# One core, attention and experts: single score banks, a fourth maxima bank, and the row maxima transposed on VectorE

## The chip, the cores and the metric

The kernel runs on 1 core of one Trainium2 chip. Its time is the device time of one execution in microseconds (us). Before the change it takes 2506.57 us, the median of 3 runs (2504.11 to 2506.87). The engines are TensorE (PE in the profile), VectorE (DVE), ScalarE (ACT), GpSimd (POOL) and SyncE (SP), which issues most DMAs. PEld is TensorE's weight load.

## The reference, cut to what matters

The input x is 8 sequences of 1024 tokens with 256 features. It is normalised, goes through attention with 16 heads of 16 features (with a linear position bias) and through a mixture of 8 experts (two per token) plus a shared one, and everything is added to x:

```
xn = layernorm(x)
scores = einsum('bqhd,bkhd->bhqk', Q, K) * scale + alibi
attn = softmax(scores); out = einsum('bhqk,bkhd->bqhd', attn, V) @ Wo + bo
y = sum over the two best experts of w * (silu(xn @ W1) * (xn @ W2)) @ W3  + shared expert
result = x + out + y
```

All of it is float32 with a softmax that subtracts each query's largest score.

## The kernel before, in words

The program is one list of steps (class `Order`), and each engine walks the same list and emits its own part of each step. So the order of `Order.run` and `Order.attention` is the order of every queue. Between engines there are semaphores only.

Stages: layernorm and the projections (to about 210 us), attention (to about 1530 us), the experts in 71 blocks of 256 slots (to about 2130 us), then the shared expert and the output.

Attention goes over 64 pairs of heads (8 sequences, 8 pairs). A pair takes 4 rows of `ORDERS`, one for every two chunks of 128 keys. In a row, `S` is a score matmul (a chunk of 128 keys against 512 queries of one head, with the bias and the negative row maximum as extra contraction rows), `u` a maxima matmul (128 queries against 512 keys), and `P` a third of the values matmuls of the row before. S and u of neighbouring positions use different halves of TensorE's rows and run beside each other. Per pair there are 32 S, 32 u and 12 P.

The maxima run ahead of the scores by `AHEAD` units, because a query's largest score must be known before its exponentials. VectorE reduces each u (`reduce_max`, 128x512 to 128x1, L944), then folds the 32 numbers of a pair to 16 (L948); GpSimd negates them and splits them in a high and a low part (L1215 to L1220, tile `mneg`, 128x32). `max_rows` brings these 128x32 numbers to rows 52 and 53 of each head's query operand `QO`: TensorE transposes them (L503) into a score bank, ScalarE copies them out to `mT` (L788), and SyncE issues two DMAs of 16 pieces of 512 B (L1399). The first S of the next pair waits for these DMAs (semaphores `mx0`, `mx1`).

PSUM has 8 banks of 512 columns. Before, banks 0 to 3 hold scores in two groups of two (both heads; ScalarE takes 1024 columns in one exponential, L799), bank 4 the values, banks 5 to 7 the maxima.

SyncE's queue in a pair, in order: `sq<-accs` (L1410, waits for ScalarE's copy of the last pair's values, L806, at the end of row 0), the 12 loads of the operands of the pair three later (L1389) and their 4 bias rows (L1393), `OTd<-accs` (L1422), the maxima's DMAs (L1399), `Sd<-sq` (L1414), and after that has landed `asum<-Sd` (L1418).

In pairs 0 to about 25 VectorE has two more steps a pair for the routing of tokens. In pairs 34 to 49 GpSimd scatters the tokens with indirect DMAs.

Of the kernel before, what the change touches and what calls it, by code (L numbers as in the profile page):

```python
# [36 lines left out]
AHEAD = 52  # L37
# [6 lines left out]
ORDERS = ("SuSuSuPSuSuSuPSuSuP", "SuSuSuPSuSuPSuSuSuP", "SuSuPSuSuSuPSuSuSuP", "SuSuPSuSuSuPSuSuSuP")  # L44
# [9 lines left out]
    "xt qkmm vmm mxmm mrt smm pv rtmm sct gmm up down sdn "  # L54

    "wsplh woh xh qkh vev mrev exp acc1 rte wsh sch sg hh yev och "

    "wspll bq wol st ag ve norm xl qkl mxred m16 rcp rt rtm rtd rtw rts rtp rtc wslv scl hf hl ocl s1 gf fin "
# [17 lines left out]
class Order:  # L76
# [3 lines left out]
    def run(self):  # L80
# [17 lines left out]
        for g in range(NG):  # L98
# [29 lines left out]
            if n >= 32 and not rows0:  # L128
                self.max_rows(0, 7)
                rows0 = True  # L130
# [80 lines left out]
    def attention(self, s, n):  # L211

        r, kc = divmod(s, 8)
        if s % 2 == 0:
            i = v = 0
            for c in ORDERS[kc // 2]:
                if c == "S":
                    if r < NPAIR:
                        self.scores(r, kc + i // 4, i % 2, i // 2 % 2)
                    i += 1  # L220
                elif c == "u":
                    if n < 32 * NPAIR:
                        self.max_unit(n)
                        n += 1
                else:
                    if v == 1 and kc == 4 and r + 1 < NPAIR:
                        self.max_rows(r + 1)
                    if s >= 2:
                        self.values(*divmod(s - 2, 8), v)
                    v += 1  # L230
# [6 lines left out]
        if s % 2 and s // 2 < NBLK:  # L237
            self.clear_slots(s // 2, 16 * r + 2 * kc)
        if SCAT_AT <= r < SCAT_AT + NG:
            self.scatter_rows(r - SCAT_AT, kc, 16 * r + 2 * kc)  # L240
# [34 lines left out]
    def max_rows(self, r, bank=None): pass  # L275
# [29 lines left out]
class Ring(Order):  # L305
# [14 lines left out]
    def bank(self, what, i):  # L320
        return 5 + self.turns.index((what, i)) % 3
# [10 lines left out]
def build(nc, t, out):  # L332
    ctx = ExitStack()
    with ctx:
# [43 lines left out]
        mT = sbuf(ctx, "mT", [32, 2, P], F32R)  # L378
# [106 lines left out]
        class Tensor(Order):  # L485
# [57 lines left out]
            def ring_bank(self, what, i):  # L543

                at = ring.turns.index((what, i))
                if at >= 3:
                    was, j = ring.turns[at - 3]
# [4 lines left out]
                else:  # L552
                    self.w.wait_ge("vev", 4 * NG)
                    if at == 2:
                        self.w.wait_ge("mxred", ring.turns[0][1])
                return 5 + at % 3

            def max_unit(self, n, bank=None):
                r, u = divmod(n, 32)
                hh, i, half = 1 - u % 2, u // 4, u // 2 % 2  # L560
# [4 lines left out]
                else:  # L565
                    self.w.wait_ge("mxred", n)
                    if n >= 32:
                        self.w.wait_ge("mrev", 1)
# [3 lines left out]
            def max_rows(self, r, bank=None):  # L572
                self.w.wait_ge("mnl", r + 1)
                self.w.wait_ge("c_ident", 16)
                if bank is None:
                    bank = 1
                    self.w.wait_ge("exp", 16 * (r - 1) + 9)
                else:
                    self.w.wait_ge("mxred", 32)
                self.turn(ps[0:32, bank, 0:P],  # L580
                          mneg[:, r % 2, :, :, :].rearrange("p h l i -> p (h l i)")).then_inc(sem["mrt"], 1)

            def scores(self, r, kc, hh, half):
                k, h0, n = r % 4, 64 * hh, 16 * r + 2 * kc + half
                bank = 2 * (n % 2) + hh
                self.w.wait_ge(f"op{k}", 256 * (r // 4 + 1))
                self.w.wait_ge(f"mx{r % 2}", 32 * (r // 2 + 1))
                if n < 2:
# [3 lines left out]
                if kc == 5 and half == 0 and hh == 1:  # L592
                    self.w.wait_ge("mrev", min(r + 2, NPAIR))
                q = self.mm(ps[:, bank, :], KO[h0:h0 + KEXP, k, kc * P:(kc + 1) * P],
                            QO[h0:h0 + KEXP, k, half * GT:(half + 1) * GT], True, True)
                if hh == 1:
                    q.then_inc(sem["smm"], 1)

            def values(self, r, kc, v):
# [3 lines left out]
                for c in range(kc, kc + 2):  # L603
# [4 lines left out]
                    self.w.wait_ge("exp", n + 2)  # L608
                    self.w.wait_ge("vcp", 2 * b + 2)
                    if c == 0:  # L610
                        self.w.wait_ge("acc1", r)
                        self.w.wait_ge("vev", 4 * NG)
                    for hh in range(2):
                        for half in range(2):
                            g4 = 2 * hh + half
                            done = self.mm(ps[32 * g4:32 * g4 + 32, 4, at],
                                           vb[:, b % 2, c, 32 * (2 * j + hh):32 * (2 * j + hh) + 32],
                                           pt(n + half)[:, hh * GT:(hh + 1) * GT][:, at], c == 0 and v == 0,
# [16 lines left out]
            def slot_columns(self, b):  # L635
                k = b % 2
                self.w.wait_ge(f"xs{b % 4}", 16 * (b // 4 + 1))
                if b < 2:
                    self.w.wait_ge("exp", 16 * NPAIR)
# [11 lines left out]
            def block_up(self, b, hc):  # L651
# [8 lines left out]
                if n < 4:  # L660
                    self.w.wait_ge("exp", 16 * NPAIR)
# [78 lines left out]
        class Scalar(Order):  # L740
# [43 lines left out]
            def max_rows(self, r, bank=None):  # L784
                bank = 1 if bank is None else bank
                self.w.wait_ge(f"mx{r % 2}", 32 * (r // 2))
                self.w.wait_ge("mrt", r + 1)
                self.e.copy(mT[:, r % 2, :], ps[0:32, bank, 0:P]).then_inc(sem["mrev"], 1)  # L788

            def scores(self, r, kc, hh, half):  # L790
                if hh == 0:
                    return
                n = 16 * r + 2 * kc + half
                b = 2 * (n % 2)
                if n % NPT >= NPT // 2:
                    projections_over(self.w)
                self.w.wait_ge("pv", n // 2 - 3)
                self.w.wait_ge("smm", n + 1)
                self.e.activation(pt(n), ps[:, b:b + 2, :], ACT.Exp).then_inc(sem["exp"], 1)  # L799

            def values(self, r, kc, v):
                if kc == 6 and v == 2:
# [3 lines left out]
                    self.e.copy(accs[:, r % 2, :], ps[:, 4, :]).then_inc(sem["acc1"], 1)  # L806
# [67 lines left out]
        class Vector(Order):  # L874
# [648 lines left out]
```

## Time and profile before

| | |
|---|---|
| median of 3 runs | 2506.57 us |
| the profiled execution's own time | 2505.09 us |
| its span | 2503.3 us |
| PE busy | 2456.3 us (98%) |
| DVE busy | 2052.1 us (82%) |
| ACT busy | 1658.8 us (66%) |
| POOL busy | 843.7 us (34%) |
| chain that ended last | PE 93%, ACT 3%, issue 1%, DVE 1%, DMA 1% |
| granted TensorE clock, mean | 0.993 |

Busy time is the union of an engine's instruction spans. TensorE's matmuls overlap and their ends are modelled, so its busy share near 100% doesn't say that it ran without waits; the start-to-start times in the timeline say more. A timeline's row stands for several like instructions in a row, with the start of the first, the time from there to the end of the last, and their count.

### The profile page before, as it was taken

The page shows a single profiled execution, that of the slowest core. Times are in us where ns is not written, and L with a number is a line of the kernel's source. Part 1 is how long each engine was busy: PE and PEld are TensorE (multiplying, and loading weights), DVE is VectorE, ACT ScalarE, POOL GpSimd, SP SyncE. Part 2 cuts the span into 40 slices and gives each one's busy share as a digit, 9 for nine tenths or more (in the row PEclk, how much of TensorE's full clock was granted, in tenths as well). Part 3 has the DMA queues.
Part 4 walks back from the last instruction along what each step waited for, and adds up shares of the span by engine and source line. Part 5 has one row for each costly group of instructions (what it writes and reads, how often), then busy time and mean ns, then how long its engine had stood idle before and what let it go on. Part 6 is the DMA issues. An engine that isn't in the chain of part 4 may idle for free.

```text
span 2503.3 us, 51165 instructions
## 1 busy us (share of the span) xinstructions
PE 2456.3 (98%) x20186; PEld 1649.2 (66%) x20186; DVE 2052.1 (82%) x3521; ACT 1658.8 (66%) x2314; POOL 843.7 (34%) x929
## 2 busy tenths in 40 slices
PE   6999999999999999999999998999999999999999
PEld 5775444444444444444444445999999988888887
DVE  7977999999999999999999993777777765554444
ACT  3445777787788888888888887777777753333222
POOL 3332332332101115555411112333333334444444
PEclk9998999999999999999999999999999999999999
DMA  8985443544222235555422233777777743444332
GB/s 285 339 298 177 153 142 122 161 145 140 76 68 78 80 85 160 157 154 154 147 76 76 75 118 105 237 237 239 239 241 241 242 152 102 121 117 116 102 102 85
DMA packets 213599, 384.41 MB, mean 154 GB/s; under 512 B 45444, under 2 KB 134724, under 8 KB 203988
## 3 DMA queue, kind: packets, MB, share of 16 engines
q1 hardware_dynamic: 175088, 218.25, 28.3%
q0 software_dynamic: 37184, 162.09, 20.4%
q8 instruction: 160, 2.62, 0.4%
q10 hardware_dynamic: 1088, 0.79, 0.1%
q14 instruction: 79, 0.65, 0.1%
HBM read 249.10 MB, written 141.49 MB: 156 GB/s over the span
## 4 chain that ended last, share of the span: by engine, by line
PE 93%; ACT 3%; issue 1%; DVE 1%; DMA 1%; SPq 0%; POOL 0%; ACTq 0%; DVEq 0%; POOLq 0%
PE ps L490 91%; PE ps L503 3%; ACT pta L799 1%; ACT ptb L799 0%; ACT mT L788 0%; DMA Wvst<-in_Wg 0%; ACT qkH L775 0%; SPq L1389 0%; DVE qkL L934 0%; DMA xr<-Xn 0%; DVE xn L918 0%; DVE XL L926 0%; DMA OPS<-Alid 0%; POOL vs L1183 0%; DVE VB L1083 0%
## 5 line engine op out<-in xcount | busy, mean ns | idle before, releaser
L944 DVE TENSOR_REDUCE mx<-ps 128x1 f32<-128x512 f32 x2048 | 1262.0, 680 | 34.6 <-PE ps L490 19.0
L490 PE MATMUL ps<-OPS 52*128 52x512 f32 (+1 forms) x4096 | 821.2, 452 | 9.5 <-ACT pta L799 1.8
L490 PEld LDWEIGHTS ps<-OPS 54*128 54x128 f32 (+1 forms) x4096 | 426.4, 186 | 507.9 <-issue 203.9
L799 ACT ACTIVATE pta<-ps 128x1024 f32<-128x1024 f32 x512 | 510.4, 1023 | 150.8 <-PE ps L490 143.4
L799 ACT ACTIVATE ptb<-ps 128x1024 f32<-128x1024 f32 x512 | 510.9, 1024 | 116.5 <-PE ps L490 116.2
L490 PE MATMUL ps<-OPS,WB 128*128 128x256 f32 (+1 forms) x2268 | 363.5, 312 | 2.9 <-DVE VB L1083 1.6
L490 PEld LDWEIGHTS ps<-OPS,WB 128*128 128x128 f32 x2268 | 310.5, 180 | 32.3 <-issue 3.3
L490 PE MATMUL ps<-pta,VB 128*32 128x352 f32 (+1 forms) x4096 | 302.6, 390 | 0.0
L490 PE MATMUL ps<-ptb,VB 128*32 128x352 f32 (+1 forms) x4096 | 301.4, 389 | 0.0
L1227 POOL TENSOR_TENSOR accs<-accs,asum 128x512 f32<-128x512 f32 x64 | 81.7, 1277 | 586.7 <-DMA asum<-Sd 561.6
L490 PE MATMUL ps<-OPS,WB0c 128*128 128x256 f32 (+3 forms) x1440 | 257.9, 330 | 3.8 <-issue 2.8
L490 PEld LDWEIGHTS ps<-OPS,WB0c 128*128 128x128 f32 (+1 forms) x1440 | 210.2, 181 | 33.8 <-issue 4.6
L490 PE MATMUL ps<-WB,OPS 128*128 128x256 f32 (+1 forms) x1422 | 188.1, 283 | 0.0
L1088 DVE TENSOR_TENSOR OPS<-VB,OPS 128x256 fp32r<-128x256 f32 (+1 forms) x213 | 151.2, 710 | 33.6 <-ACT OPS L841 33.6
L490 PEld LDWEIGHTS ps<-WB,OPS 128*128 128x128 f32 (+1 forms) x1422 | 178.4, 191 | 0.1
L865 ACT ACTIVATE VB<-ps 128x512 f32<-128x512 f32 (+1 forms) x96 | 57.0, 594 | 174.1 <-PE ps L490 174.1
L490 PEld LDWEIGHTS ps<-pta,VB 128*32 128x32 f32 x4096 | 94.1, 109 | 99.8 <-issue 84.2
L490 PEld LDWEIGHTS ps<-ptb,VB 128*32 128x32 f32 x4096 | 94.2, 109 | 99.6 <-issue 90.3
L871 ACT CAST OPS<-VB 128x512 fp32r<-128x512 f32 (+1 forms) x96 | 59.6, 621 | 138.2 <-DVE VB L1112 138.2
L1309 POOL DMA_INDIRECT gath<-Ys,slot x128 | 132.9, 1038 | 36.4 <-issue 34.1
L841 ACT CAST OPS<-VB 128x256 fp32r<-128x256 f32 (+1 forms) x213 | 86.5, 406 | 83.6 <-DVE VB L1083 83.4
L1267 POOL DMA_INDIRECT Xs<-xr,slot x128 | 125.8, 983 | 44.5 <-PE ps L490 25.2
(155 smaller groups left out, 2755.0 us busy)
## 6 DMA issues: line engine op xcount, KB each, us to landing
OPS<-QKh SPq DMA_DIRECT2D x512, 64.0 KB
Xs<-zero POOLq DMA_DIRECT2D x71, 256.0 KB, 3.3
xr<-Xs SPq DMA_DIRECT2D x71, 256.0 KB, 5.3
Ys<-VB SPq DMA_DIRECT2D x71, 256.0 KB, 5.0
QKh<-qkH SPq DMA_DIRECT2D x16, 1024.0 KB, 7.2
QKl<-qkL SPq DMA_DIRECT2D x16, 1024.0 KB, 8.9
OPS<-QKl SPq DMA_DIRECT2D x256, 64.0 KB
asum<-Sd SPq DMA_DIRECT2D x64, 256.0 KB
```

The lines of the kernel that those rows point to most:

```text
L490: return self.e.matmul(o, l, r, start=start, stop=stop)
L503: return self.e.transpose(o, in_, ident[:, :])
L799: self.e.activation(pt(n), ps[:, b:b + 2, :], ACT.Exp).then_inc(sem["exp"], 1)
L841: self.e.copy(HH[0:hn, s, 0:BT], hfq[0:hn, k, :]).then_inc(sem["hh"], 1)
L865: self.e.activation(sg[0:hn, k, :], ps[0:hn, 2 + 2 * (n % 2), :], ACT.Silu).then_inc(sem["sg"], 1)
L871: self.e.copy(HH[0:hn, s, :], hf[0:hn, k, :]).then_inc(sem["hh"], 1)
L944: e.reduce_max(mx[:, k2, hh, i, half:half + 1], ps[:, bank, :], AX.X).then_inc(sem["mxred"], 1)
L1088: e.tensor_tensor(HL[0:hn, s, 0:BT], hfq[0:hn, k, :], HH[0:hn, s, 0:BT].bitcast(F32), ALU.subtract).then_inc(sem["hl"], 1)
L1227: self.e.tensor_tensor(accs[:, r % 2, :], accs[:, r % 2, :], asum[:, :], ALU.mult).then_inc(sem["nrm"], 1)
L1267: e.indirect_dma_start(Xs[:, :], bass.IndirectOffsetOnAxis(ap=slot[:, c, 4 * g + j:4 * g + j + 1], axis=0), xr[:, k, j, :], None).then_inc ...
L1309: self.e.indirect_dma_start(gath[:, j, c, :], None, Ys[:, :], bass.IndirectOffsetOnAxis(ap=slot[:, c, i:i + 1], axis=0)).then_inc(sem[f"ga ...
```

## The change

- The scores use three single banks, 0 to 2. Each S has its own semaphore count and its own exponential of 512 columns, so there are 2048 exponentials where there were 1024, and S number n waits for the exponential of n-3.
- The values move to bank 3, the maxima get banks 4 to 7.
- The order in a row: S now goes through a head's two query halves first and then to the other head; u the same the other way round. One `ORDER` for all four rows in place of four. `AHEAD` goes from 52 to 56.
- Of a pair's 16 couples of u, four (`DOUBLE`) are reduced over two neighbouring banks in one instruction, 128x1024 to 128x2.
- The transposition of `mneg` goes from TensorE and ScalarE to VectorE (`transpose`, 32x32 blocks, SBUF to SBUF), at the first P of the third row where it was the second. The result lies in four blocks of partitions, so that SyncE issues eight DMAs of 16 pieces of 128 B in place of two of 16 pieces of 512 B.

```
-ORDERS = ("SuSuSuPSuSuSuPSuSuP", "SuSuSuPSuSuPSuSuSuP", "SuSuPSuSuSuPSuSuSuP", "SuSuPSuSuSuPSuSuSuP")
+ORDER = "SuSuSuPSuSuSuPSuSuP"
+DOUBLE = (2, 6, 10, 14)
...
-                        self.scores(r, kc + i // 4, i % 2, i // 2 % 2)
+                        self.scores(r, kc + i // 4, i // 2 % 2, i % 2)
...
-                    if v == 1 and kc == 4 and r + 1 < NPAIR:
+                    if v == 0 and kc == 4 and r + 1 < NPAIR:
                         self.max_rows(r + 1)
...
-        mT = sbuf(ctx, "mT", [32, 2, P], F32R)
+        mT = sbuf(ctx, "mT", [P, 2, 32])
...
             def scores(self, r, kc, hh, half):
...
-                self.w.wait_ge("exp", n - 1)
...
+                self.w.wait_ge("exp", n - 2)
+                self.mm(ps[:, n % 3, :], KO[h0:h0 + KEXP, k, kc * P:(kc + 1) * P],
+                        QO[h0:h0 + KEXP, k, half * GT:(half + 1) * GT], True, True).then_inc(sem["smm"], 1)
...
-                self.e.activation(pt(n), ps[:, b:b + 2, :], ACT.Exp).then_inc(sem["exp"], 1)
+                self.e.activation(pt(m)[:, half * GT:(half + 1) * GT], ps[:, n % 3, :], ACT.Exp).then_inc(sem["exp"], 1)
...
+                if u // 2 not in DOUBLE or n < AHEAD:
+                    self.w.wait_ge("mxmm", n + 1)
+                    self.e.reduce_max(mx[:, r % 2, hh, i, half:half + 1], ps[:, bank, :], AX.X).then_inc(sem["mxred"], 1)
+                elif half:
+                    self.w.wait_ge("mxmm", n + 1)
+                    self.e.reduce_max(mx[:, r % 2, hh, i, :], ps[:, bank - 1:bank + 1, :], AX.X).then_inc(sem["mxred"], 2)
...
+            def max_rows(self, r):
+                self.w.wait_ge("mnl", r + 1)
+                self.w.wait_ge(f"mx{r % 2}", 128 * (r // 2))
+                self.e.transpose(mT[:, r % 2, :], mneg[:, r % 2, :, :, :].rearrange("p h l i -> p (h l i)")
+                                 ).then_inc(sem["mtr"], 1)
...
-            def max_rows(self, r, bank=None):
-                self.w.wait_ge("mrev", r + 1)
+            def max_rows(self, r):
+                self.w.wait_ge("mtr", r + 1)
                 for hh in range(2):
-                    self.e.dma_start(QO[64 * hh + 52:64 * hh + 54, r % 4, :].bitcast(F32).rearrange("l (i n) -> l i n", n=P),
-                                     mT[16 * hh:16 * hh + 16, r % 2, :].bitcast(F32)).then_inc(sem[f"mx{r % 2}"], 16)
+                    for b in range(4):
+                        c0 = 32 * b + 16 * hh
+                        self.e.dma_start(QO[64 * hh + 52:64 * hh + 54, r % 4, :].bitcast(F32)
+                                         .rearrange("l (i b n) -> l b i n", i=8, b=4)[:, b, :, :],
+                                         mT[c0:c0 + 16, r % 2, :]).then_inc(sem[f"mx{r % 2}"], 16)
```

On SyncE, in the middle of attention, the queue before, from the last loads of a pair to the first of the next (`OPS` is the tile that holds `QO`):

```order
L1389 DMA OPS<-QKh 16x1024 x4
L1389 DMA OPS<-QKl 16x1024 x2
L1393 DMA OPS<-Alid 2x1024 x2
L1422 DMA OTd<-accs 128x512
L1399 DMA OPS<-mT 2x8x128 x2
L1414 DMA Sd<-sq 128x16
L1418 DMA asum<-Sd 128x1x512
L1410 DMA sq<-accs 128x1x16
```

And the same stretch of SyncE's queue now:

```order
L1374 DMA OPS<-QKh 16x1024 x4
L1374 DMA OPS<-QKl 16x1024 x2
L1378 DMA OPS<-Alid 2x1024 x2
L1410 DMA OTd<-accs 128x512
L1386 DMA OPS<-mT 2x8x32 x8
L1402 DMA Sd<-sq 128x16
L1406 DMA asum<-Sd 128x1x512
L1398 DMA sq<-accs 128x1x16
```

The maxima's DMAs stand at the same place, behind the loads and `OTd<-accs`; there are eight where there were two, and each keeps its 16 pieces.

On VectorE, a pair in the second half of attention before (`mx` takes the reductions, `m` the fold to 16, `sq` belongs to the sums of the softmax):

```order
L948 TENSOR_REDUCE m<-mx 128x16
L944 TENSOR_REDUCE mx<-ps 128x1 x12
L953 RECIPROCAL sq<-sq 128x16
L944 TENSOR_REDUCE mx<-ps 128x1 x20
L948 TENSOR_REDUCE m<-mx 128x16
```

And a pair now:

```order
L932 STREAM_TRANSPOSE mT<-mneg 128x32
L919 TENSOR_REDUCE mx<-ps 128x1
L922 TENSOR_REDUCE mx<-ps 128x2
L919 TENSOR_REDUCE mx<-ps 128x1 x2
L938 RECIPROCAL sq<-sq 128x16
L919 TENSOR_REDUCE mx<-ps 128x1 x4
L922 TENSOR_REDUCE mx<-ps 128x2
L919 TENSOR_REDUCE mx<-ps 128x1 x6
L922 TENSOR_REDUCE mx<-ps 128x2
L919 TENSOR_REDUCE mx<-ps 128x1 x2
L926 TENSOR_REDUCE m<-mx 128x16
```

The fold moves to the end of a pair's first row, four units earlier against the scores; one transposition is new; and of each row's eight units the fifth and sixth are one instruction.

## Rows read from the trace of the kernel before

**Rows 1.** The page, part 1: busy time and share of the span
```profile
PE 2456.3 (98%) x20186; PEld 1649.2 (66%) x20186; DVE 2052.1 (82%) x3521; ACT 1658.8 (66%) x2314; POOL 843.7 (34%) x929
```
**Rows 2.** Timeline of PE, 800 to 840 us: start, length, engine, instructions, count
```profile
804.87 1.24 PE L490 MATMUL ps<-OPS 54*128 54x512 f32 x6
806.04 0.80 PE L490 MATMUL ps<-ptb,VB 128*32 128x352 f32 x8
806.77 1.08 PE L490 MATMUL ps<-OPS 54*128 54x512 f32 x6
807.78 0.75 PE L490 MATMUL ps<-ptb,VB 128*32 128x160 f32 x16
808.46 0.74 PE L490 MATMUL ps<-OPS 54*128 54x512 f32 x4
809.13 0.80 PE L490 MATMUL ps<-ptb,VB 128*32 128x352 f32 x8
...
817.26 0.28 PE L503 MATMUL ps<-ident,mneg 128*32 128x128 f32 x1
817.47 0.75 PE L490 MATMUL ps<-ptb,VB 128*32 128x160 f32 x16
...
825.06 1.25 PE L490 MATMUL ps<-OPS 54*128 54x512 f32 x6
```
**Rows 3.** Timeline of DVE, 800 to 840 us
```profile
800.65 12.24 DVE L944 TENSOR_REDUCE mx<-ps 128x1 f32<-128x512 f32 x20
812.92 0.19 DVE L948 TENSOR_REDUCE m<-mx 128x16 f32<-128x32 f32 x1
813.03 7.73 DVE L944 TENSOR_REDUCE mx<-ps 128x1 f32<-128x512 f32 x12
820.67 0.24 DVE L953 RECIPROCAL sq<-sq 128x16 f32<-128x16 f32 x1
```
**Rows 4.** Timeline of DVE, 821.9 to 822.5 us
```profile
821.38 1.27 DVE L944 TENSOR_REDUCE mx<-ps 128x1 f32<-128x512 f32 x2
```
**Rows 5.** Timeline of ACT, 808 to 812 us
```profile
810.16 0.58 ACT L806 COPY accs<-ps 128x512 f32<-128x512 f32 x1
810.64 1.03 ACT L799 ACTIVATE ptb<-ps 128x1024 f32<-128x1024 f32 x1
```
**Rows 6.** Timeline of SP, 810 to 843 us: its DMA issues
```profile
810.77 0.57 SPq L1410 DMA_DIRECT2D sq<-accs  x1
...
814.22 0.57 SPq L1393 DMA_DIRECT2D OPS<-Alid  x2
814.83 2.91 SPq L1389 DMA_DIRECT2D OPS<-QKh  x4
...
819.71 1.36 SPq L1399 DMA_DIRECT2D OPS<-mT  x2
...
835.10 1.92 SPq L1389 DMA_DIRECT2D OPS<-QKh  x4
...
839.00 1.37 SPq L1399 DMA_DIRECT2D OPS<-mT  x2
```
**Rows 7.** SP's waits, 740 to 900 us: us in total, times, longest
```profile
SPq L1418 <- DMA Sd<-sq: 13.1, 8, 2.6
```
**Rows 8.** SP's waits, 900 to 1250 us
```profile
SPq L1418 <- DMA Sd<-sq: 35.4, 18, 3.0
```
**Rows 9.** Line 1399: issue time in ns (min/median/max), first and last start
```profile
L1399 SPq DMA_DIRECT2D OPS<-mT x128: 616/654/810, 173.7 to 1504.5; - x128
```
**Rows 10.** DVE's groups by shape, whole run: busy us, mean ns of one
```profile
L974 DVE TENSOR_TENSOR r_o<-r_t,r_r 128x512 f32<-128x512 f32 x2 | 1.4, 680 | 0.0
...
L926 DVE TENSOR_TENSOR XL<-ps,XH 128x1024 fp32r<-128x1024 f32 x16 | 19.4, 1212 | 5.4 <-ACT XH L766 5.4
```
**Rows 11.** Timeline of DVE, 236 to 282 us, pairs with routing steps
```profile
253.06 0.24 DVE L953 RECIPROCAL sq<-sq 128x16 f32<-128x16 f32 x1
...
274.43 0.24 DVE L953 RECIPROCAL sq<-sq 128x16 f32<-128x16 f32 x1
```

More of the change, by code:

```diff
@@ L35 @@
 EPS = 1e-5
-AHEAD = 52
+AHEAD = 56
 FIRST = 5
@@ L127, in run @@
                 self.spread_v(0, g - V_AT)
-            if n >= 32 and not rows0:
-                self.max_rows(0, 7)
+            if n >= 36 and not rows0:
+                self.max_rows(0)
                 rows0 = True
@@ L215, in attention @@
             i = v = 0
-            for c in ORDERS[kc // 2]:
+            for c in ORDER:
                 if c == "S":
                     if r < NPAIR:
-                        self.scores(r, kc + i // 4, i % 2, i // 2 % 2)
+                        self.scores(r, kc + i // 4, i // 2 % 2, i % 2)
                     i += 1
@@ L274, in max_unit, with max_rows @@
     def max_unit(self, n, bank=None): pass
-    def max_rows(self, r, bank=None): pass
+    def max_rows(self, r): pass
     def load_v(self, b, f): pass
@@ L320, in bank @@
     def bank(self, what, i):
-        return 5 + self.turns.index((what, i)) % 3
+        return 4 + self.turns.index((what, i)) % 4
 def rows(w):
@@ L545, in ring_bank @@
                 at = ring.turns.index((what, i))
-                if at >= 3:
-                    was, j = ring.turns[at - 3]
+                if at >= 4:
+                    was, j = ring.turns[at - 4]
                     if was == "max":
@@ L615, in values @@
                             g4 = 2 * hh + half
-                            done = self.mm(ps[32 * g4:32 * g4 + 32, 4, at],
+                            done = self.mm(ps[32 * g4:32 * g4 + 32, 3, at],
                                            vb[:, b % 2, c, 32 * (2 * j + hh):32 * (2 * j + hh) + 32],
-                                           pt(n + half)[:, hh * GT:(hh + 1) * GT][:, at], c == 0 and v == 0,
+                                           pt(n + hh)[:, half * GT:(half + 1) * GT][:, at], c == 0 and v == 0,
                                            c == 7 and v == 2)
@@ L782, in project_v @@
                 self.e.copy(vs[:, k, j, :], ps[:, bank, 0:D + NE]).then_inc(sem["vev"], 1)
[L784 to L788, printed above, removed]
-            def scores(self, r, kc, hh, half):
[L791 to L795, printed above, removed]
+            def scores(self, r, kc, hh, half):
+                m, n = 16 * r + 2 * kc + hh, 32 * r + 4 * kc + 2 * hh + half
+                if m % NPT >= NPT // 2:
                     projections_over(self.w)
-                self.w.wait_ge("pv", n // 2 - 3)
+                self.w.wait_ge("pv", m // 2 - 3)
                 self.w.wait_ge("smm", n + 1)
-                self.e.activation(pt(n), ps[:, b:b + 2, :], ACT.Exp).then_inc(sem["exp"], 1)
+                self.e.activation(pt(m)[:, half * GT:(half + 1) * GT], ps[:, n % 3, :], ACT.Exp).then_inc(sem["exp"], 1)
             def values(self, r, kc, v):
@@ L805, in values @@
                     self.w.wait_ge("pv", 8 * (r + 1))
-                    self.e.copy(accs[:, r % 2, :], ps[:, 4, :]).then_inc(sem["acc1"], 1)
+                    self.e.copy(accs[:, r % 2, :], ps[:, 3, :]).then_inc(sem["acc1"], 1)
             def route(self, i):
```

61 lines of the change are left out of this document (20 added, 41 removed).

## The prediction

> **What bounds the kernel now.** I read the page's busy shares first: PE 98% and DVE 82% over the whole span, ACT 66% [rows 1]. They mix stages. The change touches attention alone, so I went to one pair of heads in the timelines. PE begins the first S of a pair at 804.87 and of the next at 825.06 [rows 2]: a period of 20.2 us, 64 times.
>
> What each engine needs in it, by start-to-start times:
>
> - PE [rows 2]: a P of 352 columns takes 0.73 (806.04 to 806.77), six matmuls without a wait 1.01 (806.77 to 807.78), a P of 160 columns 0.68, four matmuls 0.67 (808.46 to 809.13). A row is 2 x 1.01 + 0.67 + 2 x 0.73 + 0.68 = 4.83, a pair 19.3, and the transposition 0.2 (817.26 to 817.47): 19.5.
> - DVE [rows 3]: 20 reductions in 12.27 (800.65 to the fold at 812.92, 0.61 each), the fold 0.11, 12 reductions in 7.64 (0.64 each), the reciprocal 0.16: 20.2, the whole period. DVE has no gap. But two reductions in a row that nothing holds last 1.27, of which the second's own length is 0.68 [rows 4]: 0.59 from start to start, 0.60 in round numbers. So 32 of them need 19.2, and some 0.7 us a pair are small waits for PE, too short to show as gaps since neighbouring spans overlap.
> - ACT: 16 exponentials of 1024 columns and a copy; it idles a third of the span [rows 1].
>
> So the period is DVE's, with PE 0.7 behind and small waits between them. It is so in the pairs with routing too: the reciprocals at 253.06 and 274.43 lie 21.4 apart [rows 11], and two more steps of up to 0.68, as this one [rows 10], stand in each.
>
> The reader should then look at a queue that no busy share shows: SP's. After `sq<-accs` (810.77, which waits for ACT's copy that ended at 810.74 [rows 5]) SP issues 12 loads, 4 bias rows and `OTd<-accs` without pause, and reaches the maxima's two DMAs at 819.71, and in the next pair at 839.00 [rows 6]. They hold it 1.36 together. The first S of the next pair waits for them to land. No row has that landing; the nearest is `Sd<-sq`, also 8 KB, whose landing SP waits for 13.1 us in 8 times, 1.6 each [rows 7], and 35.4 in 18, 2.0 each, while GpSimd scatters [rows 8]. So they land at 821.07 + 1.6 = 822.7, 2.4 us before S at 825.06; in the next pair at 840.37 + 1.6 = 842.0, 3.2 us before S at 825.06 + 20.2. That spare time, 2.8 us on average, is what the change meets.
>
> **The change part by part.**
>
> Eight DMAs for two on SP. Six more, in the one place where everything behind is waited for. One costs what it holds SP: 0.62 to 0.81, median 0.65 [rows 9], and 1.36 for two with the gap, so 0.69 each with the next gap. The new ones have a quarter of the bytes and the same 16 pieces from 16 partitions into 2. Bounds: the cheapest issue on SP's queue is a bias row pair, 0.57 for two or 0.28 each [rows 6]; the dearest of L1399 is 0.81 [rows 9]. I take 0.69, since pieces, partitions and direction stay and only the length of a piece shrinks. Six more: 6 x 0.69 = 4.1 us. Less the spare 2.8, S comes 1.3 late. Row 0 gives back about 0.2: it needs 4.83 where it takes 4.99 now (804.87 to 809.13 and a P of 0.73 [rows 2]), and the copy waits behind an exponential of half the length. So the period is 20.2 + 1.3 - 0.2 = 21.3. This is a closed loop (S, row 0, copy, SP's queue, DMAs, S), so the delay comes back in every pair and can't be worked off by what runs ahead. In the scatter stage landing is 0.4 longer: 21.7. The one load group of 2.91 where its like takes 1.92 (814.83, 835.10) [rows 6] is in the averages; six more instructions on the queue, if such holds come by instruction, add 0.1.
>
> [...]
>
> DVE. Four couples a pair in one instruction. The nearest rows are a 128x512 operation of 0.68 and a 128x1024 one of 1.21 [rows 10]: 0.53 per 512 columns, so a double takes 0.60 + 0.53 = 1.13 for 1.20, 0.07 saved, 0.3 a pair. Bounds: nothing, and 0.60 each if the second bank were free, 2.4 a pair. The Trainium skill's price for one DVE access to PSUM (Perfetto Trace Analysis, Optimizing Scalar/DVE Operations) is about 125 ns, which would make it 0.5 a pair; the measured start-to-start less the columns' 0.53 leaves 0.07 here. Added is the transposition, 32 columns: between the fold's 0.11 and the reciprocal's 0.24 [rows 3], taken as 0.13. DVE's need is 24 x 0.60 + 4 x 1.13 + 0.11 + 0.16 + 0.13 + 0.1 (the fold waits for the last reduction) = 19.4. Beside a period of 21.3 none of it counts.
>
> PE. The transposition goes, 0.2 a pair, and its wait. The order of S and u still gives each position both halves of the array; I cost it at nothing, bounds -0.1 and +0.1 a row. PE's own need is 19.3, hidden too.
>
> ACT. 32 exponentials of 512 columns. A 512-column copy takes 0.48 to the next start (810.16 to 810.64) [rows 5], so 15.4, and 0.48 for the copy: 15.9 of 21.3. Hidden; upper bound 0.58 each, the copy's full length, 18.6 with the copy, hidden still. Three single banks: an S writes about 0.5, is read 0.58, and its bank is due again 1.7 us later (two groups on), so no wait there.
>
> A fourth maxima bank removes most of the small waits between PE and DVE, 0.5 a pair, and `AHEAD` 56 puts four more reductions ahead of the first S, 4 x 0.6 = 2.4 us once, of which DVE's later lead gives nothing back when SP bounds. At the end 56/32 pairs run without maxima; there single banks let S and exponentials overlap where groups of two alternate: 0 to 20.2 - 15.9 = 4.3 a pair, 0 to 7.5 in all, 4 taken.
>
> The transposition's wait for GpSimd's `mnl` holds DVE's queue, but the fold is 2 rows earlier, so it is over. It runs 11 to 12 us after the pair's start, before SP is there (13.9 to 14.8 us).
>
> **The sum**, against the profiled execution (2505.09):
>
> - 18 pairs outside routing and scatter: 18 x 1.1 = +20.
> - 19 pairs with scatter or other bulk traffic (34 to 50, and 60 and 61, where the experts' first loads begin): 19 x 1.5 = +28.
> - 24 pairs with routing, period 21.4 now, 21.3 by the loop, DVE 19.4 + 1.2 = 20.6: 0.
> - more holds on the queue, 37 x 0.1 = +4; start +2; end -4.
>
> Together +50: 2555 by the profiled execution, 2556 by the median, which is 1.5 above it.
>
> **Rivals.**
>
> A. The short DMAs are cheap to issue (like the bias rows, 0.28, 0.33 with the gap). Then 6 x 0.33 - 2.8 is below nothing, the loop isn't closed, and the period is PE's and DVE's: 19.4, with some waits 19.6. 37 x 0.6 + 24 x 0.7 + 4 - 2 = 41 gained: 2465. At 0.42, as a load of 16 pieces (four in 1.92 [rows 6] at the most 0.48 each with the gap), 8 issues take 3.7 and the period is about 19.6 to 20: 2480. [...] Against: L1399 held SP 0.62 even at its least [rows 9]. The change is slower than now from about 0.55 an issue on, and that is the point that decides between the sides.
>
> B. Break-even: issues of 0.5 to 0.55 eat just what DVE and PE gain: 2495 to 2515.
>
> C. The landing grows as well, since eight small DMAs queue behind each other and behind the scatter's traffic (longest wait 3.0 against 2.0 on average [rows 8]): 1 us more in 61 pairs, 2615.
>
> D. The loop is as forecast, but the copy and the loads start later than now because a stalled PE restarts at a lower clock. Nothing in the rows speaks for it; I leave it in C's chance.
>
> **How the numbers follow.** Forecast 0.72, A 0.15, B 0.06, C and D 0.07. The forecast's own range is 2530 to 2590: issue 0.65 to 0.75 with its gap, landing 1.3 to 2, which is 0.5 a pair either way in 61 pairs. With the others the range is 2490 to 2600. This kernel's measurement can tell 0.2% (5 us) from no change. Faster by more: A and half of B, 0.17. Within: 0.03. Slower: 0.80.
>
> **What would show it.** In the profile after: eight `OPS<-mT` issues of about 0.65 in a row, some 5.5 us; PE's first S of a pair waiting for the DMA, with 1 to 2 us idle, in pairs of about 21.3; DVE's busy share in attention down from 98% to near 90%; double reductions of about 1.21 length; exponentials of about 0.6. It would be wrong if the eight take under 4 us, or if the period is below 20 with DVE without gaps; and the loop would be wrong if PE waits for maxima or exponentials instead.

## The result, and the profile after

The changed kernel takes 2536.73 us, the median of 4 runs (2527.61 to 2542.31), where the kernel before, run beside it, takes 2505.34 (2502.41 to 2506.87). The ratio is 1.0123, with a 95% interval of 1.0091 to 1.0156: slower, as forecast (2556, range 2490 to 2600), though by 31 us and not by 50. The profiled execution took 2534.91 us, its span is 2532.7, and the granted TensorE clock is 0.982 on average where it was 0.993.

The page, part 1, answers to [rows 1]; part 4 is the chain that ended last, first by engine and then by line; the last row is the score and maxima matmuls' group of part 5:

```profile
PE 2418.7 (95%) x20122; PEld 1590.6 (63%) x20122; DVE 2027.7 (80%) x3336; ACT 1711.2 (68%) x3274; POOL 841.3 (33%) x929
...
PE 58%; SPq 27%; DMA 5%; ACT 4%; issue 4%; DVE 2%; POOL 0%; ACTq 0%; DVEq 0%; POOLq 0%
PE ps L491 55%; SPq L1374 12%; SPq L1386 10%; DMA OPS<-mT 5%; SPq L1378 2%; PE ps L504 2%; ACT pta L774 2%; ACT accs L781 1%; SPq L1398 1%; SPq L1410 1%; DVE mx L919 1%; DMA Wvst<-in_Wg 0%; DVE qkL L909 0%; ACT qkH L759 0%; DVE XL L901 0%
...
L491 PE MATMUL ps<-OPS 52*128 52x512 f32 (+1 forms) x4096 | 787.5, 456 | 80.6 <-DMA OPS<-mT 76.6
```

Before, PE had 93% of the chain and SP's queue no share worth a row. Now SP's queue has 27%, 12% of it in the loads (L1374) and 10% in the eight DMAs of the maxima (L1386), and PE sat idle 76.6 us for the maxima's DMAs.

One quiet pair (without routing steps and scatter) of SP's queue, to be laid beside [rows 6] (start, length, engine, line, operation, tiles, count):

```profile
806.01 0.34 SPq L1410 DMA_DIRECT2D OTd<-accs  x1
806.39 5.24 SPq L1386 DMA_DIRECT2D OPS<-mT  x8
811.73 0.34 SPq L1402 DMA_DIRECT2D Sd<-sq  x1
...
818.30 0.57 SPq L1398 DMA_DIRECT2D sq<-accs  x1
...
825.90 0.34 SPq L1410 DMA_DIRECT2D OTd<-accs  x1
826.29 5.28 SPq L1386 DMA_DIRECT2D OPS<-mT  x8
```

And PE at the start of that pair and of the next, which answers to [rows 2] (in brackets the idle time ahead of it and what ended it):

```profile
811.40 0.80 PE L491 MATMUL ps<-pta,VB 128*32 128x352 f32 x8
812.77 0.96 PE L491 MATMUL ps<-OPS 54*128 54x512 f32 x6 [0.57 <-DMA OPS<-mT]
813.66 0.80 PE L491 MATMUL ps<-ptb,VB 128*32 128x352 f32 x8
...
817.50 0.96 PE L491 MATMUL ps<-OPS 54*128 54x512 f32 x6
...
832.74 0.97 PE L491 MATMUL ps<-OPS 54*128 54x512 f32 x6 [0.91 <-DMA OPS<-mT]
```

The loop can be read off these rows. S at 812.77, `sq<-accs` at 818.30, the loads, the first of the eight at 826.29 (13.52 after S), the last over at 831.57, S at 832.74. The period is 19.97. The eight hold the queue 5.28 where the two held it 1.36. From the end of the last issue to S are 1.14 and 1.17 us. In the trace's semaphore events S starts 0.04 us after the last of the DMAs has landed, in each of the 38 pairs 24 to 61 (pairs are counted from 0).

VectorE in the same pair, for [rows 3] and [rows 4]:

```profile
805.17 0.20 DVE L932 STREAM_TRANSPOSE mT<-mneg 128x32 f32<-128x32 f32 x1
805.29 0.65 DVE L919 TENSOR_REDUCE mx<-ps 128x1 f32<-128x512 f32 x1
805.86 1.22 DVE L922 TENSOR_REDUCE mx<-ps 128x2 f32<-128x1024 f32 x1
806.99 1.28 DVE L919 TENSOR_REDUCE mx<-ps 128x1 f32<-128x512 f32 x2
...
813.33 2.48 DVE L919 TENSOR_REDUCE mx<-ps 128x1 f32<-128x512 f32 x4 [0.24 <-PE ps L491]
```

A double takes 1.13 from start to start (805.86 to 806.99), the transposition 0.12. VectorE, which had no gap in these rows before, now has one at the start of each pair: it waits for TensorE, which waits for SP.

So far the quiet stage. Most of the loss is elsewhere. The periods by stage, from the first S of a pair to the first S of the next, on average, in both traces:

| pairs | before | after | difference in the span |
|---|---|---|---|
| to the first S | 211.3 | 209.2 | -2 |
| 0 to 25, with routing | 21.32 | 20.93 | -10 |
| 25 to 34, quiet | 20.19 | 20.28 | +1 |
| 34 to 51, scatter | 20.19 | 22.45 | +38 |
| 51 to 60, quiet | 20.18 | 20.38 | +2 |
| the last pairs and the rest | | | 0 |

Of the 10 us gained in the routing pairs, 3.7 are one pair's: number 8 took 25.45 us before (386.31 to 411.76) and 21.73 after, since the kernel before ran a part of it at half of the clock and the kernel after did not. Nothing here shows that the change did this: in experiment 4 the same pair takes 26.25. The stretch (length, then busy time and instructions of PE, PEld, DVE, ACT, POOL, then the granted clock, the DMA engines' share and GB/s):

```profile
391.00:397.00 6.00, 6.00 (x40) 2.41 (x43) 3.76 (x7) 3.26 (x5) 1.75 (x3) 0.50 0.58 216
```

Two stretches of the kernel after, in the same columns:

```profile
740.00:880.00 140.00, 133.36 (x1344) 56.46 (x1344) 135.06 (x217) 120.40 (x231) 16.60 (x33) 1.00 0.28 77
...
1000.00:1100.00 100.00, 90.12 (x844) 38.34 (x842) 85.92 (x135) 75.31 (x145) 46.13 (x57) 0.91 0.44 135
```

The same of the kernel before:

```profile
740.00:880.00 140.00, 139.26 (x1343) 65.64 (x1347) 137.72 (x237) 113.55 (x126) 17.15 (x32) 1.00 0.27 77
...
1000.00:1100.00 100.00, 99.59 (x949) 46.92 (x949) 98.42 (x169) 81.22 (x90) 55.10 (x68) 1.00 0.50 151
```

In the scatter stage the granted clock falls to 0.91; before, it was 1.00 in every stretch that I compared from 740 us on. What happens there shows in the first row of a pair, at 1093.81, on PE, and in the windows for most of that row:

```profile
1093.81 1.65 PE L491 MATMUL ps<-OPS 54*128 54x512 f32 x6 [2.50 <-DMA OPS<-mT]
1095.38 1.40 PE L491 MATMUL ps<-ptb,VB 128*32 128x352 f32 x8
...
1101.99 1.49 PE L491 MATMUL ps<-OPS 54*128 54x512 f32 x6
1103.42 0.80 PE L491 MATMUL ps<-pta,VB 128*32 128x352 f32 x8
...
1119.76 1.27 PE L491 MATMUL ps<-OPS 54*128 54x512 f32 x6 [3.12 <-DMA OPS<-mT]
```
```profile
1094.00:1102.00 8.00, 8.00 (x50) 2.96 (x50) 5.28 (x8) 4.23 (x8) 0.01 (x1) 0.50 0.09 33
```

After a stall of 2.50 us the same six matmuls take 1.57 to the next start where they take 0.89 at 812.77, and the P of 352 columns 1.33 for 0.73. The granted clock is 0.50 there, the lower of TensorE's two levels, 1.2 GHz. The first row takes 8.18 us (1093.81 to 1101.99) instead of 4.73 (812.77 to 817.50). Of the pairs from 25 on, 13 have such a first row, of 6.1 to 8.2 us. Each came after a stall of 1.8 us or more; the 26 others had none or a stall of up to 2.0.

This goes round the loop: a late S makes a stall, the stall a slow row 0, the slow row a late copy of the values, and this a late queue and a late S. In the 17 scatter pairs `sq<-accs` begins 20.5 us later after S, in sum, than at the usual 5.53, and the DMAs land 15.8 us later, in sum, than in the usual 1.09. These two make 36 us, where the table has 38.

### The profile page after: what moved, and what is told of

Same layout as the page of the kernel before. It is cut to its first block, busy times and chain, and to the rows that moved or that the text cites. A ratio compares the mean times of both kernels' runs of the same rounds, so it can differ in the third digit from the quotient of the medians.

```text
span 2532.7 us, 52382 instructions
## 1 busy us (share of the span) xinstructions
PE 2418.7 (95%) x20122; PEld 1590.6 (63%) x20122; DVE 2027.7 (80%) x3336; ACT 1711.2 (68%) x3274; POOL 841.3 (33%) x929
## 4 chain that ended last, share of the span: by engine, by line
PE 58%; SPq 27%; DMA 5%; ACT 4%; issue 4%; DVE 2%; POOL 0%; ACTq 0%; DVEq 0%; POOLq 0%
PE ps L491 55%; SPq L1374 12%; SPq L1386 10%; DMA OPS<-mT 5%; SPq L1378 2%; PE ps L504 2%; ACT pta L774 2%; ACT accs L781 1%; SPq L1398 1%; SPq L1410 1%; DVE mx L919 1%; DMA Wvst<-in_Wg 0%; DVE qkL L909 0%; ACT qkH L759 0%; DVE XL L901 0%
## 5 line engine op out<-in xcount | busy, mean ns | idle before, releaser
L919 DVE TENSOR_REDUCE mx<-ps 128x1 f32<-128x512 f32 x1550 | 972.1, 680 | 89.5 <-PE ps L491 87.9
L491 PE MATMUL ps<-OPS 52*128 52x512 f32 (+1 forms) x4096 | 787.5, 456 | 80.6 <-DMA OPS<-mT 76.6
L491 PEld LDWEIGHTS ps<-OPS 52*128 52x128 f32 (+1 forms) x4096 | 371.5, 189 | 558.6 <-ACT pta L774 207.6
L774 ACT ACTIVATE pta<-ps 128x512 f32<-128x512 f32 x1024 | 540.8, 597 | 193.0 <-PE ps L491 182.0
L774 ACT ACTIVATE ptb<-ps 128x512 f32<-128x512 f32 x1024 | 535.7, 600 | 57.6 <-PE ps L491 52.4
L491 PE MATMUL ps<-ptb,VB 128*32 128x352 f32 (+1 forms) x4096 | 312.6, 402 | 0.0
L922 DVE TENSOR_REDUCE mx<-ps 128x2 f32<-128x1024 f32 x249 | 303.2, 1218 | 3.1 <-PE ps L491 3.1
L1200 POOL TENSOR_SCALAR m<-m 128x16 f32<-128x16 f32 x64 | 16.3, 255 | 766.4 <-DVE m L926 766.4
```

The costliest lines, as they stand in the source:

```text
L491: return self.e.matmul(o, l, r, start=start, stop=stop)
L774: self.e.activation(pt(m)[:, half * GT:(half + 1) * GT], ps[:, n % 3, :], ACT.Exp).then_inc(sem["exp"], 1)
L919: self.e.reduce_max(mx[:, r % 2, hh, i, half:half + 1], ps[:, bank, :], AX.X).then_inc(sem["mxred"], 1)
L922: self.e.reduce_max(mx[:, r % 2, hh, i, :], ps[:, bank - 1:bank + 1, :], AX.X).then_inc(sem["mxred"], 2)
```

## The experiments

All are compared with the kernel before, run on the same chip; from chip to chip its median lay between 2505.0 and 2505.7. "Period" is that of the quiet pairs 25 to 34, from the trace. "With experiment 2" and the like mean that the earlier edits stay in.

**1. Are the six extra DMAs the cause? The kernel before with eight instead of two.** Each of the two is cut in four along the length of its pieces (16 pieces of 128 B); everything else stays, TensorE's transposition too, but for the two waits that count the landings (128 for 32).

```
-                    self.e.dma_start(QO[...].rearrange("l (i n) -> l i n", n=P), mT[16 * hh:16 * hh + 16, r % 2, :]...)
+                    for b in range(4):
+                        self.e.dma_start(QO[...].rearrange("l (i b n) -> l b i n", i=8, b=4)[:, b, :, :],
+                                         mT[16 * hh:16 * hh + 16, r % 2, 32 * b:32 * b + 32]...)
```

> The kernel before, where only the two maxima DMAs of 16 pieces of 512 B become eight of 16 pieces of 128 B; TensorE still transposes. Theory: eight issues of 0.66 take 5.3 us of SyncE's queue where two took 1.36, the loop closes at 20.2 + 4 - 2.8 or so, the first S of a pair waits for the maxima 0.5 to 1.5 us in a quiet pair and 2 or more in the scatter stage, and the time is 2540 to 2570, since the loop is the same as in the changed kernel and row 0 is slower. Rival (the eight DMAs are hidden, the loss is in PSUM's banks or the order): 2505 to 2510.

Measured: 2545.19 (2543.91 to 2549.05), ratio 1.016 (1.0143 to 1.0177). SP's queue in it, and what PE's weight loads waited for between 880 and 1290 us (us in total, times, longest):

```profile
820.93 5.24 SPq L1400 DMA_DIRECT2D OPS<-mT  x8
```
```profile
PEld ps L490 <- DMA OPS<-mT: 30.2, 19, 4.1
```

The period is 20.50 for 20.19, in the scatter pairs 21.85, and the clock falls to 0.96 in 880 to 1000. So six more DMAs alone turn the kernel before into one that is 40 us slower. The rest of the change, which runs with the same queue, is 8 us faster than this.

**2. Is it the place in the queue? The kernel after with half of the loads behind the maxima.** The last 8 of the pair's 16 load issues, which hold SP some 3.3 us, go behind the eight DMAs.

```
+                if kc == 4 and r + 3 < NPAIR:
+                    for i in (2, 3):
+                        self.load_pair(r + 3, i)
...
-        for i in range(4):
+        for i in range(2):
```

> The changed kernel, with the last 8 of a pair's 16 load issues (loads 2 and 3, some 3.4 us of SyncE's queue) moved behind the eight DMAs of the maxima. Theory (SyncE's queue closes a loop from the first S of a pair to the maxima's landing): the first maxima DMA starts when VectorE has transposed, about 12.1 us after the pair's first S, the last lands 5.3 + 1.1 us later at 18.5, before the 19.4 us that VectorE needs. The wait of PE for the maxima goes, the period falls from 20.2 (22.4 in the scatter stage) to 19.4 to 19.6, TensorE's clock stays at 1.0 in the scatter stage, and the time is 2450 to 2470. Rival (the loss is in the single score banks, the new order or the doubled reductions, and the wait only shows up at the pair's border): the wait moves elsewhere and the time stays at 2520 to 2540. Rival (the scatter's traffic slows the landing by itself): quiet pairs gain, the scatter pairs keep 22 us, and the time is about 2490 to 2500.

Measured: 2491.18 (2485.97 to 2496.83), ratio 0.9936 (0.9917 to 0.9954). The order of one queue is worth 46 us against the kernel after. It is less than expected: the quiet period went to 19.36, but the scatter pairs only to 20.97, with stalls and slow rows as above. The time lies in the range of the last rival, the scatter's traffic; experiments 3 and 4 will take the rest away without touching that traffic.

```profile
PEld ps L494 <- DMA OPS<-mT: 27.7, 18, 3.1
```

This is its wait for the maxima from 880 to 1290. A quiet pair of it (first S at 814.20) shows what is late next, on SP, on GpSimd and on VectorE:

```profile
818.03 0.59 SPq L1409 DMA_DIRECT2D asum<-Sd  x1
...
823.31 0.57 SPq L1381 DMA_DIRECT2D OPS<-Alid  x2
826.20 0.35 SPq L1413 DMA_DIRECT2D OTd<-accs  x1
826.60 5.28 SPq L1389 DMA_DIRECT2D OPS<-mT  x8
```
```profile
824.89 1.29 POOL L1215 TENSOR_TENSOR accs<-accs,asum 128x512 f32<-128x512 f32 x1 [4.11 <-DMA asum<-Sd]
```
```profile
826.22 0.20 DVE L935 STREAM_TRANSPOSE mT<-mneg 128x32 f32<-128x32 f32 x1
```

SP is done with the bias rows at 823.88, but `OTd<-accs` begins only at 826.20, when GpSimd's multiplication has ended (824.89 + 1.29). GpSimd had stood idle for `asum<-Sd`, the load of the softmax's sums, and this is a price of the edit itself: the load stands behind the late loads now and goes out 3.8 us after S, where in the kernel after it went out 0.4 after S. And the transposition, at the third row's first P, isn't over before 826.42. So the eight begin 12.8 us after S in the quiet pairs, on average, only 1.0 earlier than in the kernel after. These two are what experiments 3 and 4 move.

**3. The transposition two P earlier**, at the second row's second P (with experiment 2).

```
-                    if v == 0 and kc == 4 and r + 1 < NPAIR:
+                    if v == 1 and kc == 2 and r + 1 < NPAIR:
```

> As e1_late_loads, and the transposition stands in the pair's second row (second P) instead of the third, so that the maxima's DMAs start about 10 us after the first S and land at 16.4, some 3 us before they are wanted. Theory: the same period of 19.4 in quiet pairs, and no wait in the scatter pairs even where the landing takes 3 us; time 2445 to 2460, 0 to 15 under e1_late_loads. Rival (VectorE waits for GpSimd's split of the maxima, since the fold ends only 5.5 us after the first S and GpSimd needs 1 us and may be in a DMA): VectorE loses 0.3 to 1 us a pair, and the time is 2470 or more.

Measured: 2467.38 (2465.19 to 2468.61), ratio 0.9849 (0.9833 to 0.9866): 24 us faster than experiment 2, but 7 above the expected range. The quiet period is 19.28, so VectorE lost nothing there. Pairs 39 to 51 still take 19.9 to 21.3, 20.6 on average. SP's queue there:

```profile
1002.52 0.57 SPq L1381 DMA_DIRECT2D OPS<-Alid  x2
1005.91 0.35 SPq L1413 DMA_DIRECT2D OTd<-accs  x1
1006.31 5.24 SPq L1389 DMA_DIRECT2D OPS<-mT  x8
```

And GpSimd, whose result `OTd<-accs` stores, there and one pair later:

```profile
1004.61 1.28 POOL L1215 TENSOR_TENSOR accs<-accs,asum 128x512 f32<-128x512 f32 x1 [5.22 <-PE ps L494]
1006.05 1.07 POOL L1255 DMA_INDIRECT Xs<-xr,slot  x1 [0.16 <-issue]
...
1024.73 1.28 POOL L1215 TENSOR_TENSOR accs<-accs,asum 128x512 f32<-128x512 f32 x1 [5.45 <-DMA asum<-Sd]
```

SP is done with the bias rows at 1003.09 and starts `OTd<-accs` at 1005.91, when GpSimd's multiplication has ended (1004.61 + 1.28). For 2.8 us the store that nobody is in a hurry for holds the eight that TensorE needs. GpSimd isn't late because it is busy with the scatter, as the expectation of experiment 4 has it: it stands idle for over 5 us ahead of the multiplication. In the program this step waits for `asum<-Sd` alone, and a pair later the profile names it. By the start of the multiplication this load landed 7.3 us after its issue here (997.29 to 1004.61) and 4.9 in a quiet pair (859.80 to 864.66), so the scatter's traffic may well be at the root; no run takes it alone.

**4. The normalisation and its store behind them too** (with experiment 3).

```
+                if kc == 4 and 2 <= r < NPAIR:
+                    self.heads(r - 2, 3)
...
-        if r >= 2:
+        if r >= NPAIR:
```

> As e5_early_transpose, and GpSimd's normalisation of the pair two back with SyncE's OTd<-accs moved from the pair's first row to behind the loads of the third row, so that on SyncE's queue nothing that waits for GpSimd stands ahead of the maxima's DMAs. Theory (in e5's pairs 39 to 52 the eight DMAs started at 1006.3 us since OTd before them waited for GpSimd, which was busy with the scatter, and so the loop closed through GpSimd): the periods there fall from 20.2 to 20.7 to 19.3, 13 pairs by about 1.2 us, and the time is 2445 to 2455. Rival (the scatter's traffic holds the landing or SyncE itself): no change, 2463 to 2470.

Measured: 2455.63 (2455.43 to 2457.68), ratio 0.9805 (0.9788 to 0.9821), the fastest of all, faster than both kernels, and 0.6 above the expected range. Its windows:

```profile
740.00:880.00 140.00, 140.00 (x1398) 63.49 (x1396) 139.76 (x225) 125.33 (x240) 17.34 (x32) 1.00 0.28 80
...
1000.00:1100.00 100.00, 100.00 (x1004) 45.14 (x996) 99.83 (x163) 89.53 (x173) 55.43 (x68) 1.00 0.54 163
```

The clock is back at 1.00 in the scatter stage, VectorE has no gap in the timeline (it is busy 139.76 of 140), the eight begin some 9.7 us after S, and the period is 19.28 on average in the pairs 25 to 60, scatter or not, in none of them over 19.5. Nothing was done to the clock or to the scatter; the stalls went, and the lower level with them.

**5. Is the scatter itself the cause of the falling clock? The kernel after with the scatter from pair 43 on**, run once.

```
-SCAT_AT = 34
+SCAT_AT = 43
```

> The changed kernel with the scatter of tokens in pairs 43 to 58 instead of 34 to 49. Theory (the scatter's traffic lengthens the landing, PE then stands still for over 2 us, and restarts at a lower clock): the long periods of 22 to 26 us and the clock under 1.0 move to these pairs, pairs 35 to 42 run at 20.2 with the clock at 1.0, and the time stays at 2525 to 2545. Rival (something else in that stretch of time, whatever is in the kernel): the long periods stay at 915 to 1290 us.

Measured: 2543.3, a single execution, so only its trace is read here. Three of its stretches:

```profile
880.00:1000.00 120.00, 113.07 (x1082) 47.18 (x1078) 110.15 (x176) 96.92 (x185) 13.14 (x24) 0.94 0.28 75
1000.00:1100.00 100.00, 94.72 (x916) 40.08 (x912) 91.96 (x148) 81.91 (x158) 10.33 (x21) 0.95 0.27 75
...
1290.00:1490.00 200.00, 178.29 (x1684) 74.81 (x1682) 171.78 (x273) 151.32 (x290) 89.34 (x109) 0.93 0.44 135
```

The long periods, mostly 22 to 24 us, moved with the scatter (now 22.88 in pairs 51 to 60). But half of my theory fell: from 880 to 1100, where nothing is scattered now (75 GB/s), the clock is 0.94 to 0.95 all the same, with periods of 20.5 to 22.5. Every second pair has a slow first row, after stalls of 1.6 to 2.3 us. So the scatter isn't needed for it. What it adds is the later landing, and so longer stalls: S comes 1.1 to 1.2 us after the last issue in these pairs, and up to 3.5 where the scatter runs. Why the slow rows begin near 880, when a pair at 792 had a stall of 1.7 us and an ordinary row, stays open.

**6. What are the doubles worth? Experiment 4 without them.**

```
-DOUBLE = (2, 6, 10, 14)
+DOUBLE = ()
```

> As e7_late_otd, with no doubled reductions: all 32 of a pair are single. Theory (VectorE bounds the pair at 19.3 us, and a doubled reduction saves 0.60 x 2 - 1.13 = 0.07 us): 0.27 us a pair more, 62 pairs, 15 to 18 us over e7_late_otd. Rival (PE bounds at 18.9 to 19.3, VectorE is beside it): within 5 us of e7_late_otd. Rival (a doubled reduction holds both banks and so costs PE more waits than it saves): faster than e7_late_otd.

Measured: 2471.42 (2469.83 to 2471.96), ratio 0.9867 (0.9851 to 0.9884): 15.8 us slower than with them, a period of 19.54 for 19.28. VectorE is again without a gap, so this is its own time: 0.26 for four, 0.065 each. Both rivals fall.

**7. And the fourth maxima bank? Experiment 6 with three**, and the waits for a free bank to match.

```
-        return 4 + self.turns.index((what, i)) % 4
+        return 4 + self.turns.index((what, i)) % 3
```

> As e8_no_double, with the maxima in three banks (4 to 6) as before the change, bank 7 unused. Theory (the fourth bank takes away the small waits between PE and VectorE of 0.5 to 0.7 us a pair that made up the difference between 32 x 0.60 and the period before): the period goes from 19.55 to about 20.1, 25 to 40 us over e8_no_double. Rival (the small waits came from the two groups of two score banks, which are gone): within 8 us of e8_no_double.

Measured: 2499.1 (2496.93 to 2501.12), ratio 0.9978 (0.9969 to 0.9988): 27.7 us slower than with four, a period of 20.05. VectorE in it, then in experiment 6:

```profile
818.94 9.91 DVE L924 TENSOR_REDUCE mx<-ps 128x1 f32<-128x512 f32 x16
828.88 0.19 DVE L931 TENSOR_REDUCE m<-mx 128x16 f32<-128x32 f32 x1
```
```profile
808.65 9.59 DVE L924 TENSOR_REDUCE mx<-ps 128x1 f32<-128x512 f32 x16
818.27 0.19 DVE L931 TENSOR_REDUCE m<-mx 128x16 f32<-128x32 f32 x1
```

Sixteen reductions take 9.91 with three banks and 9.59 with four. The waits between them are too short to show as gaps in either; VectorE's busy time from 740 to 880 us has a part of them, 138.73 against 139.72. The kernel of this experiment has no doubles and no fourth bank. It is still 6 us faster than the kernel before, by what is left of the change together with the new queue.

**8. Would the queue's order alone have helped the kernel before?** Experiments 2 and 4 on it, nothing else (the same two edits).

> The kernel before with SyncE's queue in the order of e7_late_otd (late loads and late OTd<-accs behind the maxima's two DMAs), and nothing else. Theory (before the change the maxima land 2 to 4 us before they are wanted, so the queue's order is worth nothing there): 2500 to 2508, no difference. Rival (the queue's order helps by itself, through the loads or the softmax's sums, whatever the maxima do): faster by 10 us or more.

Measured: 2510.67 (2506.26 to 2517.48), ratio 1.0031 (1.0018 to 1.0044). No gain, but a loss of 6 us, 3 above the expected range; the period is 20.19 as before, and the routing pairs take 21.52 for 21.32. Why these lose stays open. Where two DMAs stand at the queue's end with some 3 us to spare, their place is worth nothing.

**9. Every other couple doubled**, eight of a pair's sixteen where experiment 4 has four: if four save 16 us, do eight save 32?

```
-DOUBLE = (2, 6, 10, 14)
+DOUBLE = (0, 2, 4, 6, 8, 10, 12, 14)
```

> As e7_late_otd, with eight of a pair's 16 couples reduced in one instruction instead of four. Theory (VectorE still bounds the pair, at 19.28): another 4 x 0.07 less, 19.0 us a pair, near the 18.9 that four first rows of 4.72 make for PE; 12 to 17 us under e7_late_otd, 2438 to 2444. Rival (PE is the bound by then, or the second doubled reduction of a row meets units that are not there yet): 0 to 8 us under e7_late_otd, or slower.

Measured: 2467.89 (2466.99 to 2471.76), ratio 0.9855 (0.9838 to 0.9871): 12 us slower than with four. My theory fell. VectorE's transpositions stand 19.53 apart (801.60 and 821.13), and from 740 to 880:

```profile
740.00:880.00 140.00, 139.86 (x1378) 61.40 (x1378) 138.07 (x195) 123.29 (x237) 18.70 (x34) 1.00 0.29 80
```
```profile
PEld ps L496 <- DVE mx L927: 4.9, 21, 0.5
```

VectorE now has gaps (138.07 for 139.76), and TensorE waits for banks that the double reductions hold, 4.9 us in 7 pairs, which experiment 4 has no row for. A double frees two banks at once and late, and needs two full ones before it starts: with four banks and a double in every other couple each side waits for the other. That this wait is the whole of the 0.25 us a pair wasn't isolated.

**10. What does an issue cost by? Eight DMAs of four pieces.** Experiment 1 with each DMA carrying 4 pieces of 512 B from 4 partitions into 1 row, where it had 16 pieces of 128 B from 16 partitions into 2.

```
+                    for b in range(4):
+                        l, q = divmod(b, 2)
+                        row, c0 = 64 * hh + 52 + l, 16 * hh + 8 * l + 4 * q
+                        self.e.dma_start(QO[row:row + 1, r % 4, 512 * q:512 * q + 512]..., mT[c0:c0 + 4, r % 2, :]...)
```

> The kernel before, with the maxima's two DMAs of 16 pieces of 512 B cut into eight of 4 pieces of 512 B (each 4 partitions into one row). It tells what an issue's price hangs on. Theory (mostly the pieces that an issue has to describe: 16 cost 0.65, the bias rows' 2 cost 0.28, so 4 cost 0.31 to 0.35): eight take 2.8 us where two took 1.36, the maxima still land before they are wanted in most pairs, and the time is 2503 to 2515. Rival (a price for each DMA whatever its pieces): eight take 5.2 us as in e3_before_eight, and the time is 2540 to 2550.

Measured: 2547.66 (2545.26 to 2550.58), ratio 1.0168 (1.0151 to 1.0185), no better than experiment 1. My theory fell, and the time is in the rival's range. The issues:

```profile
837.34 4.93 SPq L1402 DMA_DIRECT2D OPS<-mT  x8
```

Eight in 4.93, 0.62 each with the gaps between them, where with sixteen pieces of 128 B they take 5.24, 0.66 each, and two with sixteen of 512 B 1.36, 0.68 each [rows 6]. A quarter of the pieces saves 6%. So for the maxima the price is by the DMA, and the only remedy found is to issue fewer or to issue them earlier. What makes these dearer than the queue's other issues, 0.28 for a bias row pair [rows 6] or 0.34 for `Sd<-sq` from 128 partitions, no run isolates.

## Why the prediction was right, and where it was off

**What bounds the kernel: right.** SP's queue and the DMAs behind it close a loop once the maxima's issues grow. The chain of waits went from PE alone to 27% SP's queue, experiment 1 makes the loss with the DMAs alone, and experiments 2 to 4 turn it into a gain by the order of the steps alone, on SP's queue and of the transposition on VectorE's.

**The issue: right in kind, a little high.** I took 0.69 each; eight take 5.24 to 5.28, 0.66. It is 0.66 with pieces of 128 B and 0.62 with a quarter of the pieces, so pieces and bytes move it by a tenth at most. Rival A, that short DMAs are cheap to issue like the bias rows, is refuted: 0.28 holds for the bias rows and not for these.

**The period of quiet pairs: too high by 1.0.** I had 21.3, measured are 20.28 and 20.38 on average. Three terms: the eight start 13.8 after S on average in the pairs 25 to 34 (I had 14.2, the mean of 14.8 and 13.9 less 0.2, and the first of the two had a long hold in its loads), they take 5.3 (I had 5.5), and S comes 1.1 to 1.2 after (I had 1.6, from `Sd<-sq` [rows 7]). The landing was badly chosen: I took the mean of one stretch in which some of the waits were long. From 500 to 740 us the same wait of the kernel before (us in total, times, longest) is 1.1 each:

```profile
SPq L1418 <- DMA Sd<-sq: 12.4, 11, 1.3
```

That is what the maxima's landing takes too. So the 18 quiet pairs lose 3 us and not 20, and the routing pairs, where I let the loop take VectorE's gain away, gain 10, of which 3.7 are the one slow pair before.

**The scatter pairs: the loss too low by a third.** I had 21.7, a loss of 1.5 a pair, measured is 22.45 on average, 2.3 a pair, and against the quiet pairs it is +2.2 and not +0.4. The later landing is 0.9 a pair (15.8 us in 17), and the lower clock 1.2 a pair (20.5 in 17). This is rival D, of which I wrote that nothing in the rows spoke for it, and which I left in C's 0.07. TensorE never stalled in those rows. But the trace had a sign of its price that I didn't read, pair 8 above: its first row took 8.99 us where its neighbours' took 5.2. The mechanism (a stall, a restart at the lower level, row 0 longer, the loop longer) was named, its price was not worked out. Rival C's growth of the landing is there too, with the scatter only. The errors partly cancelled: 17 us too much in the quiet pairs, 10 in the routing pairs, 8 by the holds and the start, and 14 too little in the scatter and the last pairs. That the total came nearer than its parts is luck.

**VectorE: right.** The double was priced at 1.13 and takes 1.13; the saving of 0.07 each is 0.065 by experiment 6. By the Trainium skill's 125 ns for one DVE access to PSUM (Perfetto Trace Analysis, Optimizing Scalar/DVE Operations) it would have been 0.5 a pair, an estimate; measured is 0.26. The transposition takes 0.12 to 0.13 as taken. VectorE's need of 19.4 is 19.28 in experiment 4, where it is without a gap. Its busy share in the quiet stage fell to 96% (135.06 of 140) and not to near 90, as the period rose less.

**The fourth bank: right, and out of sight.** 0.5 a pair was forecast, and 0.51 is measured by experiment 7. In the kernel after it was hidden behind SP, as were the doubles.

**ScalarE: low, without effect.** Exponentials of 512 columns take 0.60 each, above my upper bound of 0.58; ScalarE is busy 120.4 of 140 us, 17 a pair and not 15.9. It is hidden behind 20 us, and behind 19.28 too.

**Where the gain went.** By experiments 6, 7 and 4 the change holds 44 us of gain (28 of the bank, 16 of the doubles), and with the steps in another order it reaches 2455.6, 49 us under the kernel before. As made it is at 2536.7: the place of the eight DMAs, behind the loads, the store and the later transposition, costs 81 us.

## What to carry to other kernels

Count a queue's issues, not its bytes, and look for the one whose landing starts the loop again: there each further DMA costs its full issue time in every turn once the spare time is used up, and what nobody waits for soon belongs behind it. When a change opens stalls on TensorE where there were none, price the restart at the lower clock as well, since a loop passes it on. For a landing, look at the spread of its rows over several stretches before taking one stretch's mean. And look at what moves with what you move: the late loads of experiment 2 made another DMA late, and with it the store.

## What the runs showed of the hardware that was not expected

- A small DMA within SBUF held SP's queue 0.66 us with 16 pieces of 128 B, 0.68 with 16 of 512 B, and 0.62 with 4 of 512 B (gaps between them included).
- In the kernel after the last of them landed 1.1 us after the end of its issue in quiet pairs, and up to 3.3 us after while GpSimd's indirect DMAs ran.
- After stalls of 1.8 to 4.0 us TensorE did up to a whole row (8.2 us instead of 4.73) at the lower level; stalls of up to 2.0 us passed without it in 24 pairs of the kernel after. In experiments 2 and 3 first rows were slow after 1.55 and 2.0, and others were not after 2.16 and 2.27. In the kernel before a row was slow from 391 us on, with no stall over 0.6 us in the 10 us ahead. So the stall's length alone doesn't decide it.
- Four double reductions a pair were 16 us faster than none; eight were 12 us slower than four.
